# One group of 21 Strassen products per pair on TensorE, and a reordered start, in a masked mixture layer followed by a top-2 expert MLP

## The reference

```python
x = x + (einsum('bnt,bot->bno', x, einsum('bg,got->bot', cond, weight * mask)) + bias)
# rw = softmax(cond); top 2 of 8 experts, their weights normalised
mlp = lambda x, g, u, d: (gelu(x @ g) * (x @ u)) @ d     # 256 -> 1024 -> 256
x = x + sum(w[k] * mlp(x, expert[k]) for k in top2) + mlp(x, shared)
```

## Time and profile before

| | |
|---|---|
| median of 3 runs | 418.2 us (418.14 to 418.57) |
| profiled execution | 416.81 us |
| its span, first to last instruction | 415.0 us |
| PE busy | 408.6 us (98%), 2241 matmuls |
| DVE, ACT, POOL busy | 296.0, 249.8, 296.4 us (71%, 60%, 71%) |
| granted PE clock | 1.00 of full speed over the whole span |

### The profile page before, as it was taken

The page is one execution under the profiler, slowest core; times in us unless marked ns, Lnnn a source line. Parts: engine busy times, 40 slices in busy tenths (PEclk is TensorE's granted clock), DMA queues, the critical chain, the costliest instruction groups (busy, mean ns, idle before and its releaser), DMA issues.

```text
span 415.0 us, 7355 instructions
## 1 busy us (share of the span) xinstructions
PE 408.6 (98%) x2241; PEld 354.5 (85%) x2241; DVE 296.0 (71%) x511; ACT 249.8 (60%) x484; POOL 296.4 (71%) x322
## 2 busy tenths in 40 slices
PE   8999999999999999999999999999999999999997
PEld 6778788888888888888888888888888888888886
DVE  3589997666667877766767878776676675666684
ACT  6576586665655567665556566666465555766541
POOL 1599899998608859989733877998661885878630
PEclk9999999999999999999999999999999999999999
DMA  7742432333200442224210053322300033232101
GB/s 249 237 141 83 126 103 80 100 101 81 74 27 0 127 127 78 77 80 129 56 42 1 24 178 84 97 97 76 101 25 25 2 100 104 76 94 86 42 10 54
DMA packets 19615, 35.23 MB, mean 85 GB/s; under 512 B 2178, under 2 KB 2946, under 8 KB 19586
## 3 DMA queue, kind: packets, MB, share of 16 engines
q1 hardware_dynamic: 19296, 34.61, 27.9%
q10 hardware_dynamic: 290, 0.26, 0.2%
HBM read 32.77 MB, written 2.10 MB: 84 GB/s over the span
## 4 chain that ended last, share of the span: by engine, by line
PE 88%; POOL 4%; DVE 4%; DMA 1%; issue 1%; SPq 1%; ACT 1%; DVEq 0%; POOLq 0%
PE o_ps L548 15%; PE p_ps L548 11%; PE g_ps L494 10%; PE g_ps L493 10%; PE g_ps L497 10%; PE u_ps L493 10%; PE u_ps L497 10%; PE u_ps L494 10%; PE l_ps L449 2%; DMA l_raw<-l_w 1%; POOL sg_lo L1154 1%; DVE l_ps L954 1%; POOL sd_lo L1185 1%; DVE h_lo L1018 1%; PE p_ps L430 1%
## 5 line engine op out<-in xcount | busy, mean ns | idle before, releaser
L1158 POOL TENSOR_TENSOR eg_lo<-raw_g,eg_hi 128x512 fp32r<-128x512 f32 x64 | 92.5, 1466 | 12.6 <-ACT eg_hi L689 12.6
L982 DVE SCALAR_TENSOR_TENSOR u_ps<-gelu,route_cur,u_ps 128x512 f32<-128x512 f32 x64 | 48.3, 754 | 54.3 <-PE u_ps L497 52.1
L718 ACT ACTIVATE gelu<-g_ps 128x512 f32<-128x512 f32 x95 | 57.2, 602 | 36.8 <-PE g_ps L497 36.3
L1018 DVE TENSOR_TENSOR h_lo<-t_raw,h_hi 128x1024 fp32r<-128x1024 f32 x46 | 67.8, 1475 | 1.1 <-ACT h_hi L746 1.1
L740 ACT CAST h_hi<-u_ps 128x512 fp32r<-128x512 f32 x46 | 27.0, 587 | 69.2 <-DVE u_ps L982 41.2
L1198 POOL TENSOR_TENSOR ed_lo<-raw_d,ed_hi 128x384 fp32r<-128x384 f32 x30 | 31.8, 1061 | 31.0 <-ACT ed_hi L698 31.0
L494 PE MATMUL g_ps<-x_hi,eg_lo 128*128 128x512 f32 (+1 forms) x128 | 50.6, 395 | 0.0
L493 PE MATMUL u_ps<-x_hi,eg_hi 128*128 128x512 f32 (+1 forms) x128 | 49.9, 390 | 0.4 <-DVE h_lo L1008 0.4
L493 PE MATMUL g_ps<-x_hi,eg_hi 128*128 128x512 f32 (+1 forms) x128 | 50.2, 392 | 0.0
L494 PE MATMUL u_ps<-x_hi,eg_lo 128*128 128x512 f32 (+1 forms) x128 | 49.8, 389 | 0.0
L746 ACT CAST h_hi<-t_raw 128x1024 fp32r<-128x1024 f32 x46 | 48.2, 1048 | 1.0 <-DVE t_raw L1004 0.9
(11 more groups left out here) (226 smaller groups left out, 1153.7 us busy)
## 6 DMA issues: line engine op xcount, KB each, us to landing
raw_g<-experts SPq DMA_DIRECT2D x64, 256.0 KB, 2.8
raw_d<-experts SPq DMA_DIRECT2D x32, 256.0 KB, 2.7
l_raw<-l_w SPq DMA_DIRECT2D x8, 256.0 KB, 5.2
x_in<-xT SPq DMA_DIRECT2D x8, 256.0 KB, 4.3
raw_g<-shared SPq DMA_DIRECT2D x8, 256.0 KB, 4.7
outT<-out_sb SPq DMA_DIRECT2D x6, 256.0 KB, 3.8
raw_d<-shared SPq DMA_DIRECT2D x4, 256.0 KB, 3.3
mask<-l_mask SPq DMA_DIRECT2D x2, 128.5 KB, 5.9
```

The lines of the kernel that those rows point to most:

```text
L718: act.activation(gelu[:, s % 2], l0_ps if at_first(b) and s == 1 else g_ps, ACT.Gelu_apprx_tanh).then_inc(gelu_done, 1)
L982: dve.scalar_tensor_tensor(u_ps[:, s % 2], gelu[:, s % 2], route_cur[:, k:k + 1], u_ps[:, s % 2], ALU.mult, ALU.mult).then_inc(h_done, 1)
L1018: dve.tensor_tensor(h_lo[:, at], t_raw[:], h_hi[:, at].bitcast(F32), ALU.subtract).then_inc(t_lo_done, 1)
L1158: pool.tensor_tensor(eg_lo[:, j % RING], raw_g[:, j % RAW_G], eg_hi[:, j % RING].bitcast(F32), ALU.subtract).then_inc(gu_lo_done, 1)
```

## The change

- PE: `down` at an even step issues nothing; at an odd step it issues products 1 to 3 and then 4 to 7, 21 matmuls in one group, behind the gate and up projection of the next odd step. The exception is the last batch's last pair of that kind (`ahead`), which keeps its two places.
- ACT and DVE: the hi and lo parts of B11 move from the even step to the odd one, in front of those of B21 and B22; only the copy of b12 stays in the even step (`copy_b12`, now behind the weights' casts). A new semaphore, `b11_read`, tells ACT that the product that reads B11 of the pair before is over; the wait for `down_done` goes to `split_b2`. On DVE the `combine` terms of odd steps move behind `form_t234`.
- The eight routing operations move from steps 3 to 6 of batch 0 to the start: four ahead of `first_x1_lo` (`route_sums`), four ahead of the first `form_h` (`route_weigh`).
- POOL's first shared sums (`shared_s(0)`) come after the third instead of the sixth half of shared weights, and `split_shared_d(0)` ahead of `split_shared(3)`. ACT's `split_shared_s(0)` comes right behind the first GELU.

```diff
@@ PE @@
-                product(P1, wt, None, A11, B11, first, last)
+                product(P1, wt, None, A11, B11, first, last).then_inc(b11_read, 1)
...
             def down(b, s):
                 if fast(b, s // 2):
-                    if s % 2 == 0:
+                    ahead = at_last(b) and s // 2 == LAST_FAST - 1
+                    if s % 2 == (0 if ahead else 1):
                         products_123(b, s // 2)
-                    else:
+                    if s % 2:
                         products_4567(b, s // 2)
@@ ACT @@
+            def copy_b12(b, p):
+                act.wait_ge(h_done, STEPS * b + 2 * p + 1)
+                if not first_pair(b, p):
+                    act.wait_ge(t_done, 4 * pair_count(b, p))
+                act.copy(b12[:], u_ps[:, 0, TH:T]).then_inc(b12_done, 1)
+
             def split_b11(b, p):
-                n = STEPS * b + 2 * p
-                act.wait_ge(h_done, n + 1)
+                act.wait_ge(t_done, 4 * pair_count(b, p) + 1)
                 if not first_pair(b, p):
-                    act.wait_ge(down_done, n - 1)
-                    act.wait_ge(t_done, 4 * pair_count(b, p))
+                    act.wait_ge(b11_read, pair_count(b, p))
                 act.copy(h_hi[:, 0:TH], u_ps[:, 0, 0:TH]).then_inc(h_hi_done, 1)
-                act.copy(b12[:], u_ps[:, 0, TH:T]).then_inc(b12_done, 1)
 
             def split_b2(b, p):
                 n = STEPS * b + 2 * p + 1
                 act.wait_ge(h_done, n + 1)
+                if not first_pair(b, p):
+                    act.wait_ge(down_done, n - 2)
                 act.copy(h_hi[:, B21 * TH:(B22 + 1) * TH], u_ps[:, 1]).then_inc(h_hi_done, 1)
...
                 elif s % 2 == 0:
+                    weights_beside(b, s)
+                    copy_b12(b, s // 2)
+                else:
                     split_b11(b, s // 2)
-                    weights_beside(b, s)
-                else:
                     split_b2(b, s // 2)
                     weights_beside(b, s)
@@ DVE, step @@
                     form_t1(b, p)
+                else:
+                    form_h(b, s)
                     split_b11(b, p)
-                else:
-                    form_h(b, s)
-                    beside(b, s, with_next)
                     split_b2(b, p)
                     form_t234(b, p)
+                    beside(b, s, with_next)
@@ DVE, start @@
+            route_sums()
             for oh in range(HH):
                 first_x1_lo(oh)
             route_index()
+            route_weigh()
@@ POOL, batch_0 @@
-                for c in range(FIRST):
-                    split_gate(c)
-                    split_up(c)
+                split_gate(0)
+                split_up(0)
+                split_gate(1)
                 shared_s(0)
+                split_up(1)
+                split_gate(2)
+                split_up(2)
+                split_shared_d(0)
                 split_shared(FIRST)
-                split_shared_d(0)
```

More of the change, by code:

```diff
@@ L186, in build @@
         t_lo_done = sem("t_lo_done")
+        b11_read = sem("b11_read")
         down_done = sem("down_done")
@@ L826, in batch @@
                     split_t(b, NP - 1)
+                    copy_b12(b + 1, 0)
+                    activate(b + 1, 1)
                     split_b11(b + 1, 0)
+                    split_b2(b + 1, 0)
                     evacuate_123(b)
-                    activate(b + 1, 1)
-                    split_b2(b + 1, 0)
                     evacuate_4567(b)
@@ L857, in _ @@
             activate(0, 0)
-            split_b11(0, 0)
+            split_shared_s(0)
+            copy_b12(0, 0)
             weights_beside(0, 0)
             activate(0, 1)
-            split_shared_s(0)
+            split_b11(0, 0)
             split_b2(0, 0)
@@ L888, in route_index @@
                     dve.max_index(top_idx[:, b], top[:, b], cond_all[:, b]).then_inc(indexed, 1)
-            def route_weigh(s):
-                if s == 3:
-                    dve.wait_ge(exp_done, 1)
-                    dve.reduce_sum(exp_sum[:], exps[:], AX_X).then_inc(weighed, 1)
-                    dve.wait_ge(weighed, 1)
-                    dve.reciprocal(exp_rsum[:], exp_sum[:]).then_inc(weighed, 1)
-                if s == 4:
-                    dve.wait_ge(weighed, 2)
-                    dve.tensor_tensor(probs[:], exps[:], exp_rsum[:].unsqueeze(2).to_broadcast([P, B, 8]), ALU.mult).then_inc(weighed, 1)
-                    dve.wait_ge(weighed, 3)
-                    dve.tensor_tensor(pair_sum[:], probs[:, :, 0], probs[:, :, 1], ALU.add).then_inc(weighed, 1)
-                if s == 5:
-                    dve.wait_ge(weighed, 4)
-                    dve.reciprocal(pair_rsum[:], pair_sum[:]).then_inc(weighed, 1)
-                    dve.wait_ge(weighed, 5)
-                    dve.tensor_tensor(pair[:], probs[:, :, 0:TOP_K], pair_rsum[:].unsqueeze(2).to_broadcast([P, B, TOP_K]), ALU.mult).then_inc(weighed, 1)
-                if s == 6:
-                    dve.wait_ge(weighed, 6)
-                    dve.tensor_scalar(pair_rest[:], pair[:], 1.0 - SCALE, None, ALU.mult).then_inc(weighed, 1)
-                    dve.wait_ge(weighed, 7)
-                    dve.scalar_tensor_tensor(route_w[:].rearrange("p (b k) -> p b k", k=TOP_K), pair[:], SCALE, pair_rest[:],
-                                             ALU.mult, ALU.add).then_inc(weighed, 1)
@@ new lines, in route_sums @@
+            def route_sums():
+                dve.wait_ge(exp_done, 1)
+                dve.reduce_sum(exp_sum[:], exps[:], AX_X).then_inc(weighed, 1)
+                dve.wait_ge(weighed, 1)
+                dve.reciprocal(exp_rsum[:], exp_sum[:]).then_inc(weighed, 1)
+                dve.wait_ge(weighed, 2)
+                dve.tensor_tensor(probs[:], exps[:], exp_rsum[:].unsqueeze(2).to_broadcast([P, B, 8]), ALU.mult).then_inc(weighed, 1)
+                dve.wait_ge(weighed, 3)
+                dve.tensor_tensor(pair_sum[:], probs[:, :, 0], probs[:, :, 1], ALU.add).then_inc(weighed, 1)
@@ new lines, in route_weigh @@
+            def route_weigh():
+                dve.wait_ge(weighed, 4)
+                dve.reciprocal(pair_rsum[:], pair_sum[:]).then_inc(weighed, 1)
+                dve.wait_ge(weighed, 5)
+                dve.tensor_tensor(pair[:], probs[:, :, 0:TOP_K], pair_rsum[:].unsqueeze(2).to_broadcast([P, B, TOP_K]), ALU.mult).then_inc(weighed, 1)
+                dve.wait_ge(weighed, 6)
+                dve.tensor_scalar(pair_rest[:], pair[:], 1.0 - SCALE, None, ALU.mult).then_inc(weighed, 1)
+                dve.wait_ge(weighed, 7)
+                dve.scalar_tensor_tensor(route_w[:].rearrange("p (b k) -> p b k", k=TOP_K), pair[:], SCALE, pair_rest[:],
+                                         ALU.mult, ALU.add).then_inc(weighed, 1)
@@ L1061, in beside @@
             def beside(b, s, with_next):
-                if at_first(b):
-                    route_weigh(s)
                 if with_next:
@@ L1111, in batch @@
                     form_t1(b + 1, 0)
+                    form_h(b + 1, 1)
                     split_b11(b + 1, 0)
-                    form_h(b + 1, 1)
                     split_b2(b + 1, 0)
```

2 lines of the change are left out of this document (1 added, 1 removed).

## The result

| | before | changed |
|---|---|---|
| median | 418.38 us (418.14 to 418.57, 4 runs) | 414.31 us (413.94 to 414.65, 4 runs) |
| profiled execution | 416.81 us, span 415.0 | 414.13 us, span 412.3 |
| ratio | | 0.9903, 95% interval 0.9886 to 0.9920 |

The two profiled executions differ by only 2.68. So two things are to be explained: 2.7 us in the profiles instead of 2.2, and 1.4 more in the timed runs than in the profiles.

A forecast was written before the change was run, and what follows sets the result against it. PE, busy all 204 us from 200 to 404, was taken as the bound, with 3.0 us of waits in batch 0. Waits -1.3 and merged gates -0.9 gave -2.2, from 418.2 to 416.0, range 414.6 to 417.3.

The forecast's parts named there:

- The group of 21: PE, all batches: 45 merged gates no longer follow products and lose 0.02 each, -0.9 us, between 0 and 1.35.
- (c): Rival, 10%: the order of matmuls costs nothing in itself, the 0.02 moves elsewhere; -1.3 alone, 416.9.
- The GELU of even steps: ACT in each steady pair: the even step's GELU ends in time for the odd gate; costed at 0.
- (e): Rival, 9%, slower: ACT reaches the even step's GELU too late, every odd gate waits; 420.5 at 0.1 beyond the margin.
- The margin of 0.66: Steady pairs: slack left between the even step's GELU on ACT and the odd gate, 1.36 - 0.60 less 0.1 hand-over.
- The start: Batch 0: waits of PE become 1.7 instead of 3.0, -1.3 us, bounds -3.0 and +0.4.
- The up of step 2: PE in batch 0: waits for DVE's lo part of B11, 0.2 late and 0.1 for a slow start, 0.3.
- the gate of step 3: PE in batch 0: waits for ACT's third GELU, 1.0 and 0.1 for the start, 1.1.
- the gate of step 5: PE in batch 0: waits for POOL's piece 5, done at 33.85, 0.3, between 0 and 1.3.
- (b): Rival, 10%: the start has almost no waits, as DVE and POOL meet less; -2.7 - 0.9, 414.6.
- (d): Rival, 11%: POOL's shared pieces come 1.0 late for each gate of steps 5 and 7; -2.2 + 1.7, 417.7.
- The end: Final sum: the median's 1.4 above the profiled 416.81 is kept as base, 418.2 - 2.2 gives 416.0.

The follow-up runs named there:

- group_inside: Changed kernel with the group of 21 between the odd gate and odd up projection in the two middle batches: 431.87 us, 1.0353 of the kernel before.
- x1_later: Changed kernel with ACT's two copies of x1 behind the third GELU instead of ahead of it: 414.49 us, 0.9912 of the kernel before.
- no_merge: Changed kernel with PE, ACT and DVE as before the merge, products in two groups: 416.20 us, 0.9951 of the kernel before.
- routing_only: Kernel before with only the routing operations moved to the start: 415.93 us, 0.9960 of the kernel before.
- routing_late: Changed kernel with the routing operations back in steps 3 to 6 of batch 0: 416.69 us, 0.9971 of the kernel before.
- merge_only: Kernel before with only the group of 21 and its moved casts; routing operations and first sums as before: 417.41 us, 0.9987.
- after_pe_code: Changed kernel with 230 more PE instructions, waits already met, in batch 0: 415.56 us, 0.9954 of the kernel before.

## Why the prediction was right and wrong

**The group of 21: right.** "I take 0.02 each": 41 merged pairs in the steady stretch gave 0.82, 0.020 each, with all 45 0.9. Gates behind up projections take 1.360, behind products 1.388. The first product of any group, of 9, 12 or 21, takes 0.113 where the others take 0.120; one group less is one such product less, which is why 0.028 shrinks to some 0.02. Rival (c) is out. The Trainium skill's "TensorE: Matmul & The Clock Gate" (section "Back-to-back issue gap") gives the gap of an isolated matmul by its own columns; by that alone the up behind products in group_inside would be no longer than another, and its 1.388 disagrees.

**The GELU of even steps: right.** No gate behind batch 0 waits for it, and (e) is out. The margin of 0.66 held, though DVE and POOL are busier by 10 and 12 us in 204.

**The start: right in its mechanism, mis-sized.** Forecast were waits of 1.7 instead of 3.0. Without waits, the stretch is 16 x 1.36 + 3 x 0.028 + 84 x 0.12 = 31.92, so 33.25 holds 1.33. The up of step 2 had 0.21 (forecast 0.3), the gate of step 3 1.01 + 0.11 (1.1), the gate of step 5 0.02 (0.3). The last is the mis-sized term: POOL was to reach the end of piece 5 at 33.85 and did so at 33.3, 0.3 of it by the first down weights already (20.32 for 20.65), the rest since its meeting with DVE's operation on T cost 0.98 (2.00 for 1.02), not 1.2. `form_h` came at 19.61 instead of 19.9; `pair` took 0.17, where each of the three operations was to wait for one of POOL's. With the 0.08 of four merged pairs in this stretch, -1.4 was forecast and -1.76 came. What I had not seen is that the gate of step 3 could be had for nothing, POOL's chain being as late (x1_later), and that the merge alone makes the early stretch slower by 1.45; the price of the first I counted rightly, but it was no lever. Rivals (b) and (d) are out. That the small operations wait for POOL's whole instruction holds, `pair_rest` with its single SBUF input too. The Trainium skill's "SBUF — State Buffer" (section "SBUF: two separate sides") names, beside two inputs, a mode of DVE with two ports as a case of exclusion. If `pair_rest` ran in that mode, which no run shows, its 0.62 agrees; my reading of the page, one input is free, was too short.

**The end: the step that failed.** "The profiled execution took 416.81 with a span of 415.0; the median is 418.2, 1.4 above it, with which I work: 416.0." I carried the 1.4 over as if it belonged to any kernel. From the profiled 416.81 the same -2.2 would have given 414.6. The 1.4 belongs to how an execution ends. A timed run is span plus 1.8 (both first profiles), and a span is head + early + steady + tail; with a head of 21.5 that is 1.8 + 21.5 + 35.03 + 355.18 = 413.5 plus the tail: 416.7 with 3.2, 418.4 with 4.9. The profiled execution had the first, the three shown runs (418.14 to 418.57) lie where the second would. For the changed kernel it is 1.8 + 21.5 + 33.26 + 354.36 = 410.9 plus 3.24: 414.2, and all its runs and repeats lie at 413.24 to 414.73. The edits' own -2.6, which steady and early show in each repeat, and -1.7 against runs with the long tail, make -4.3; the measured -4.07 is within what the heads vary by. The same sum fits the others: no_merge 414.7 or 416.4 (414.19 to 417.08), routing_only 415.5 or 417.2 (415.40 to 417.55), routing_late 416.5 (median 416.69), merge_only 417.4 (417.41).

**What is shown and what is not.** Shown: the steady 0.82, which comes with the merge in every kernel that has its group of 21 in this place; the early 1.76 and its parts; two tails 1.7 apart, and that in every long one the last 18 packets of the stores come only behind a packet of instructions; that what the longer runs of before have more lies inside their span. Argued: that it is this tail (timed runs leave no trace, and heads vary by 1.3, too), and with it that 1.4 of the 4.07 come from the tail. Open: why no profile of a kernel with the merge has the long tail, though it has not one PE instruction more; the spans of after_pe_code say that the merge doesn't rule it out. Open, too, what the 0.7 to 1.3 are that three of its runs have outside of the span.

## What to carry to other kernels

Cut every profile at a few fixed instructions and compare stretch by stretch with what repeats: here two stretches repeated to 0.03 us while the total moved by 2. If a profiled execution and the median differ by more than they vary, the difference is a state of this program, and isn't carried over to the next; forecast with both. When work between two needs of an engine is taken out, first make the producers of the second need early: the same merge cost 0.6 us net of its gain alone and was worth 0.6 net behind the other edits, most of the difference by POOL's first sums. And a wait is only worth removing if the next one behind it isn't as late already.
